# One step's 440 stages in another order: an interleaved image block on one core

## What is computed

```python
x = x + conv_block(_ln_c(x), ...)       # per 32 channels: 3x3 depthwise conv, silu, selective scan
                                        # in one of four directions, layernorm, gate, projection
t = _to_tokens(x)                       # 2304 tokens of 128 channels per image
t = t + ffn(_ln_t(t), ...)              # 16 experts; each takes its 288 best tokens (top_k)
x = _from_tokens(t, x)
```

## Time and profile before

| what | value |
|---|---|
| median of three runs | 2730.52 us |
| lowest, highest | 2722.64, 2745.78 us |
| span of the profiled execution | 2733.1 us |
| instructions in it | 41803 |
| mean granted TensorE clock, of full speed | 0.857 |

### The profile page before, as it was taken

How to read it: one execution, slowest core, us unless ns; L and a number is a source line. 1 busy time by engine, 2 the same in 40 slices (tenths; PEclk the granted TensorE clock), 3 DMA queues, 4 the chain that set the end, 5 groups by cost and what they waited for, 6 DMA issues and landing times.

```text
span 2733.1 us, 41803 instructions
## 1 busy us (share of the span) xinstructions
PE 2003.1 (73%) x12104; PEld 1220.3 (45%) x12104; DVE 1763.1 (65%) x4446; ACT 1620.9 (59%) x3141; POOL 1581.4 (58%) x1169
## 2 busy tenths in 40 slices
PE   3777788787877788786877788778878787765452
PEld 1333345454445454444545454445445454444331
DVE  2478787767676687757677777757676777664000
ACT  2456576756666576756666576757666576644221
POOL 0000366667575666757575766657575766676773
PEclk8999899999898998989898999988998998765555
DMA  3031334453635354453635454453635454444332
GB/s 109 28 89 48 83 71 93 85 130 71 139 72 126 73 108 81 87 124 72 140 72 116 85 110 79 96 120 71 138 72 127 78 110 81 79 70 81 52 64 53
DMA packets 275584, 244.85 MB, mean 90 GB/s; under 512 B 46240, under 2 KB 245264, under 8 KB 273040
## 3 DMA queue, kind: packets, MB, share of 16 engines
q0 software_dynamic: 101376, 80.29, 22.0%
q1 hardware_dynamic: 173968, 161.69, 21.0%
HBM read 83.71 MB, written 99.16 MB: 67 GB/s over the span
## 4 chain that ended last, share of the span: by engine, by line
issue 22%; DMA 15%; PE 15%; POOL 14%; SPq 10%; DVE 9%; ACT 9%; another core or an unknown queue 1%; POOLq 0%; DVEq 0%; ACTq 0%
POOL acc_dram L1035 8%; SPq L931 8%; DMA acc_dram<-Y,IDA 6%; POOL G L1016 5%; DMA slots_dram<-IX 4%; DVE hots L1437 3%; PE psum L1561 3%; PE psum L1586 2%; PE psum L1779 2%; DMA G<-rows_dram,IDX 2%; DMA GM<-rows_dram,IDX 2%; POOL acc_dram L1045 1%; SPq L964 1%; ACT hots L1168 1%; DMA LR<-slots_dram 1%
## 5 line engine op out<-in xcount | busy, mean ns | idle before, releaser
L1035 POOL DMA_INDIRECT acc_dram<-Y,IDA x512 | 860.5, 1681 | 394.3 <-issue 173.7
L1016 POOL DMA_INDIRECT G<-rows_dram,IDX x512 | 544.8, 1064 | 526.8 <-issue 429.3
L1437 DVE TENSOR_SCALAR_CACHE_REDUCE hots<-A,cand 96x384 f32<-96x384 f32 x720 | 401.7, 605 | 39.9 <-ACT A L1157 32.1
L1773 PE MATMUL psum<-m_all,G 128*128 128x128 f32 x512 | 127.9, 338 | 270.6 <-DMA G<-rows_dram,IDX 191.0
L1177 ACT ACTIVATE XG<-psum 128x256 f32<-128x256 f32 x256 | 97.5, 381 | 301.0 <-PE psum L1773 281.2
L1548 DVE TENSOR_TENSOR Y<-psum,GT 128x256 f32<-128x256 f32 x256 | 107.3, 419 | 258.7 <-PE psum L1790 206.8
L1561 PE MATMUL psum<-U,m_all 128*128 128x384 f32 x576 | 230.8, 532 | 27.3 <-DVE U L1364 17.6
L1779 PE MATMUL psum<-XG,w1s 128*128 128x256 f32 x512 | 209.1, 497 | 40.1 <-ACT PH L1202 19.6
L1561 PE MATMUL psum<-SQ,m_all 128*128 128x384 f32 x576 | 223.6, 517 | 18.8 <-ACT SQ L1074 10.0
L1045 POOL DMA_INDIRECT acc_dram<-YM,IDM x64 | 109.8, 1716 | 188.1 <-DMA acc_dram<-Y,IDA 100.5
L1773 PEld LDWEIGHTS psum<-m_all,G 128*128 128x128 f32 x512 | 65.1, 167 | 342.1 <-issue 248.2
(11 more groups left out here) (205 smaller groups left out, 4724.2 us busy)
## 6 DMA issues: line engine op xcount, KB each, us to landing
stack<-XS SPq DMA_DIRECT2D x384, 100.0 KB
rows_dram<-XT SPq DMA_DIRECT2D x16, 1296.0 KB, 7.9
X<-in_x SPq DMA_DIRECT2D x16, 1152.0 KB
acc_dram<-XT SPq DMA_DIRECT2D x16, 1152.0 KB
FT<-acc_dram SPq DMA_DIRECT2D x96, 192.0 KB
out<-OT SPq DMA_DIRECT2D x96, 192.0 KB
DH<-XS SPq DMA_DIRECT2D x96, 100.0 KB
DU<-XS SPq DMA_DIRECT2D x96, 100.0 KB
```

The lines of the kernel that those rows point to most:

```text
L1016: nc.gpsimd.indirect_dma_start(G[e % NG][:, c, :], None, rows_dram[of], bass.IndirectOffsetOnAxis(IDX[of][:, col:col + 1], 0)).then_inc(ga ...
L1035: nc.gpsimd.indirect_dma_start(acc_dram, bass.IndirectOffsetOnAxis(IDA[of][:, col:col + 1], 0), Y[e % NY][:, c, :], None, compute_op=ALU.a ...
L1437: last = v.tensor_scalar((GT1, EQ1, P1)[i], A[:], cand[:, i + 1:i + 2].bitcast(F32), 0.0, ALU.is_ge, ALU.add, accum_out=cnt[:, i:i + 1])
L1773: last = nc.tensor.transpose(bank6[:, c * FULL:(c + 1) * FULL], G[j % NG][:, c, 0:C], M["IDENT"])
```

## The change

On PE, all six parts of `conv(0)`, `layer2(0)` and `affinity_turn` now stand ahead of `conv(1, 0)`; on ACT the three `xs` stand together. The calls themselves, cut to places of which the above speaks (the full diff moves nearly every line):

```diff
+    q.lg_scale(s)
+    q.lg_shift(s)
+    q.lg_exp(s)
+    q.lg_norm(s)
+    gather(3)
     m.conv(s, 0, 0)
     m.conv(s, 0, 3)
-    q.lg_scale(s)
-    q.lg_shift(s)
...
+    gather(5)
+    scatter(3)
...
+    gather(7)
     m.dbu(s, 0)
...
-    fetch(5)
...
-    gather(15)
-    flip(4)
-    flipped(4)
-    m.tokens(s, par, 0)
-    q.store_rows(s, par)
...
     m.xm_turned(s, par, 0)
+    m.xm(s, par, 0)
+    m.xm_turned(s, par, 1)
+    q.store_rows(s, par)
...
+    scatter(12)
+    layer1(13)
+    scatter(13)
+    scatter(14)
+    scatter(15)
```

More of the change, by code:

```diff
@@ L373, in step @@
-    q.ahead(s, 4)
-    total(4)
-    m.delta(s, 0)
+    turn(2)
     decide(4)
-    m.z(s, par, 1, 0)
     q.count(s, 5, ka)
     q.ahead(s, 5)
-    m.u(s, 2)
-    m.du(s, 0)
[L382 to L386, removed]
+    m.zs(s, 1)
+    layer1(0)
+    before(0)
+    turned(2)
+    m.z(s, par, 2, 0)
+    m.du(s, 0)
     total(5)
     decide(5)
-    m.zs(s, 1)
+    layer2(2)
+    weigh(2)
+    m.z(s, par, 2, 1)
+    m.zs(s, 2)
+    q.count(s, 6, ka)
@@ L411, in step @@
+    turn(3)
+    turned(3)
+    rest(0)
+    total(7)
+    raw(0)
+    gather(5)
+    scatter(3)
+    turn_mixed(1)
+    turned_mixed(1)
+    m.spread_b(s, 0)
+    m.clamp(s, 2)
+    m.soft(s, 2)
+    q.ahead(s, 7)
+    decide(7)
+    m.delta(s, 1)
+    q.count(s, 8, ka)
+    layer1(3)
+    before(3)
+    turn(4)
+    gather(7)
     m.dbu(s, 0)
-    turn(3)
-    decide(7)
-    tables()
     m.decay(s, 0)
[L416 to L427, removed]
     layer1(2)
-    raw(0)
-    m.du(s, 1)
     before(2)
[L432 to L439, removed]
     total(8)
     turned(4)
+    layer1(4)
+    blend(0)
+    m.spread_b(s, 1)
+    q.ahead(s, 8)
+    decide(8)
     gelu(0, 2)
-    blend(0)
+    m.du(s, 1)
+    layer2(4)
+    m.scan(s, 0)
@@ L444, in step @@
+    q.count(s, 9, ka)
     summed(0)
+    scatter_mixed(0)
     m.spread_c(s, 0)
-    decide(8)
+    weigh(4)
     m.delta(s, 2)
[L448 to L453, removed]
     total(9)
-    q.ahead(s, 9)
-    weigh(4)
     layer2(5)
     m.spread_b(s, 2)
[L459 to L465, removed]
+    fetch(0)
+    gather(6)
     k2 = m.bank7()
     m.fc2(s, k2)
-    m.decay(s, 2)
+    q.ahead(s, 9)
@@ L487, in step @@
+    m.decay(s, 2)
+    m.scan(s, 1)
+    raw(1)
+    q.affinity_rows(s)
     layer1(5)
+    before(5)
+    m.sq2(s, 0)
     q.count(s, 11, ka)
-    m.sq2(s, 0)
-    raw(1)
-    m.scan(s, 2)
[L492 to L505, removed]
+    turn(6)
+    m.spread_c(s, 2)
+    scatter(4)
+    turn(7)
+    turned(6)
@@ L605, in step @@
-    turn(11)
-    before(9)
-    f.xn(nxt, other, 0)
-    kg = q.bank7()
-    q.slots_pe(s, 0, kg)
-    f.cen1(nxt, other, 2)
-    m.g(s, 2)
-    fetch(3)
+    m.g(s, 2)
+    kh0 = q.bank7()
+    q.hot(s, 0, kh0)
+    gather(13)
+    scatter(8)
+    layer2(10)
+    f.var1(nxt, 1)
+    layer1(9)
+    q.hot_scale(s, 0, kh0)
+    before(9)
+    blend(2)
+    kg0 = q.bank7()
+    q.slots_pe(s, 0, kg0)
+    weigh(10)
+    summed(2)
+    fetch(3)
+    turn(11)
+    f.xn(nxt, other, 0)
+    f.cen1(nxt, other, 2)
@@ L645, in step @@
+    turn(12)
+    turned(12)
+    gather(14)
+    layer2(11)
     layer1(12)
-    layer2(11)
+    gelu(2, 11)
+    rest(3)
+    kg1 = q.bank7()
+    q.slots_pe(s, 1, kg1)
     before(12)
-    kg = q.bank7()
-    q.slots_pe(s, 1, kg)
-    f.xs(nxt, other, 2)
-    gelu(2, 11)
-    m.xm_turned(s, par, 1)
-    m.xm(s, par, 0)
+    scale_mixed(3)
+    f.stack(nxt, other, 0)
+    weigh(11)
+    raw(3)
     m.xm_turned(s, par, 2)
+    m.xm(s, par, 1)
+    q.slots_sum(s, 1, kg1)
+    scatter(10)
+    m.xm(s, par, 2)
@@ L655, in step @@
     m.cen3(s, 0)
[L656 to L658 removed]
+    m.sq3(s, 0, last)
     m.cen3(s, 1)
[L660 to L680 removed]
+    gather(15)
@@ L724, in step @@
+    summed(3)
+    turned(14)
+    turn(15)
+    before(13)
+    turned(15)
+    m.xt(s, 0)
+    m.tokens(s, par, 1)
     m.xt(s, 1)
-    turned(14)
+    layer1(14)
+    before(14)
+    m.tokens(s, par, 2)
     m.stats(s, 0)
-    m.tokens(s, par, 2)
     m.stats(s, 1)
     m.xt(s, 2)
+    m.stats(s, 2)
+    layer1(15)
+    before(15)
+    put(4)
+    flip(5)
+    flipped(5)
+    gelu(3, 15)
+    tables()
     ks = q.bank7()
     q.slots_turn(s, ks)
-    turn(15)
-    turned(15)
     q.columns(s, par, ks)
-    layer1(14)
+    gather(16)
```

362 lines of the change are left out of this document (169 added, 193 removed).

## The result

The changed kernel takes 2521.23 us (median of 4 runs, 2515.39 to 2525.55) against 2730.72 us for the kernel before (4 runs, 2722.64 to 2745.78): a ratio of 0.923, 95% interval 0.920 to 0.926. That is 209 us less. The forecast was 2593, 140 us under the profiled span of the kernel before.

A forecast was written before the change was run, and what follows sets the result against it. No engine is busy all through a step; about 9 us in its middle and some 20 us at its end are lost to waiting. Sum: 2733 - 99 (end) - 66 (middle) + 25 (new waits) = 2593 us, range 2500 to 2724.

The forecast's parts named there:

- the two places: Waits in the middle and at the end of each step, about 9 us and some 20 us lost.
- the end: End of the step: xt's wait for the rows store goes, 7.1 us a step, 99 us; bounds 34 and 127.
- the middle: PE's and DVE's stall behind gather(6) shrinks, 5.5 us a step, 66 us; bounds nothing and 106.
- new waits: Small waits for stages a little late in PE's strict order: 25 us lost, possibly nothing or as much again.
- the rest: Steps 16 to 18, without conv block: scatter_mixed's gains by covers offset the bare scatters' losses, counted as nothing.
- My second chain: Tokens' chain to slots_turn: loses xt's 7.1 us wait; hot_scale(2), 2.49 us, now stands ahead of rstd3(0).
- c: Time from one bare scatter to the next on POOL before gather(16), taken as 7.85 us between 6.0 and 10.4.
- the formula 3c - 20.2: New middle stall per step in us if bare scatters hold gather(16): nothing below c = 6.7, 3.3 at 7.85.
- If gather(16) and the search come earlier by the same amount: Middle: gather(6) then comes 13 us earlier for the search and the 8.77 us stall is gone.
- my own list: Signs against the forecast: first count to hot(2) stays 112 us, new PE wait each step, end over 38 us.
- That of the slower kernel: Rival: bare scatters on POOL land slower still, 2786 us at c = 13.5; chance 0.1.
- All of it: Rival: both stalls, middle and end, go and nothing new comes, 2500 us; chance 0.13.

The follow-up runs named there:

- SP's order alone: Kernel before with only SP's stages in the new order (rows store ahead of the stacks, slots store right behind the second): 2637.0 us, ratio 0.964.
- the order of PE, ACT and DVE alone: Kernel before with only the stages of PE, ACT and DVE in the new order, SP and POOL in the old: 2735.9 us, ratio 1.000.
- POOL's order alone: Kernel before with only POOL's stages in the new order (gathers ahead of scatters' landings, scatters 12 to 15 before gather(16)): 2645.2 us, ratio 0.967.
- SP and POOL: Kernel before with the stages of SP and POOL in the new order, PE, ACT and DVE in the old: 2591.1 us, ratio 0.947.
- changed, gather(16) earlier: Changed kernel with gather(16) ahead of scatter(15) and gather(17) ahead of scatter_mixed(3) on POOL: 2495.9 us, ratio 0.912.

## Why the prediction was right, and where not

The sign, the range and the two places were right; the gain was 209 us where 140 were forecast. By stretches of the profiled execution, which gained 219: the end was to give 99 us and gave 149; the middle was to give 66, less 25 for new waits, and gave 61; the rest was to give nothing and gave 9. So the term that was most mis-sized is the end of the step, and half of what it gave was not in my sum.

*The end, up to slots_turn.* 373 to 300 us are 72 us, or 4.8 a step where I took 7.1, inside the bounds of 2.4 and 9.1. `xt`'s wait went and the slots store landed in 3 us, as said. What the sum had wrong is whose gain this is. "In the new order the rows store has gone ahead of the stacks", and with that I gave it to SP. SP's order alone does give 100 us, but that this is the forecast's figure is luck: its end wins 133 us and its middle loses 40. On top of POOL's order SP's is worth 54, on top of that of PE, ACT and DVE 71, and on top of both 17. I listed where `xt` went on ACT and priced `hot_scale(2)` there, but did not ask whether `xt` would still have to wait. It would not, and that alone wins nothing in this stretch: `turn(15)` then waits for gather(15), which goes out beside the rows store, and with SP's order too this wait is gone. Over the fifteen steps PE's busy time there is 328 of 372 us at a clock of 0.85 with the order of PE, ACT and DVE alone, and 280 of 293 at 1.00 with SP's order too. So 48 of these 79 us are PE's own time at another clock, a cost that my sum did not have. With POOL's order, gather(15) is issued 5 to 8 us ahead of the end of `hot(2)` instead of 7 to 10 behind it, and the stretch is 343 us without SP's order.

*The end, from slots_turn to the first count.* My second chain stopped at `slots_turn`; behind it I priced nothing. It gave 77 us, the largest single part. The order of PE, ACT and DVE alone brings this stretch from 238 to 164 us, SP's alone to 210, POOL's alone to 225. On PE `turn(15)`, layers 1 and `flip(5)` have gone from behind `slots_turn` to in front of it, and `affinity_turn` has gone ahead of conv(1, 0). Undoing the latter brings 45 of the 77 us back in this stretch. How the rest divides was not tried.

*The middle.* Gather(6) 43 us behind gather(16) was forecast, and 42.1 is the mean of 13 steps. c was taken as 7.85 us and is 6.5 on the mean in the changed kernel; with POOL's order and the rows store in its old place it is 7.6. At 6.5 the formula 3c - 20.2 gives no stall, and `hc` has none. But "If gather(16) and the search come earlier by the same amount" did not come true, and the formula, which lets gather(16) be held, has the first count too late. Means of 13 steps, in us:

| kernel | slots_turn to gather(16) | gather(16) to gather(6) | first count to gather(6) |
|---|---|---|---|
| before | 2.2 | 56.7 | 43.0 |
| SP's order alone | 2.1 | 57.9 | 45.7 |
| POOL's order alone | 9.1 | 47.1 | 40.7 |
| PE, ACT, DVE alone | 2.2 | 52.9 | 43.9 |
| SP and POOL | 13.8 | 45.8 | 46.2 |
| all: the changed kernel | 8.6 | 42.1 | 39.8 |
| changed, gather(16) earlier | 2.6 | 46.8 | 38.3 |

Behind `slots_turn` the first count comes 5.1 us earlier (10.9 us, 16.0 before) and gather(16) 6.4 us later, since it stands behind four bare scatters. So from `slots_turn` to gather(6) only 8.2 us are won of the 14.6, and from the first count to gather(6) 3.2. The formula took the first count as far behind `slots_turn` as before; with the c that was measured it has gather(6) 34.6 us (15.1 + 3c) behind the first count, and it is 39.8. With gather(16) ahead of scatter(15) another 25 us go.

*New small waits.* 25 us were taken. `over` waits 91.4 us against 72.3 and `turn_mixed` 98.8 against 37.8, and the stretch from the last count to `hot(2)` grows from 631 to 673 us (its part of the middle). The steps are 137 us long on the mean of 11, under the 140 to 146 forecast. By my own list, a new wait of several us in each step was to prove the forecast wrong; it did not, since removing it wins nothing.

*What held the step.* The forecast added terms. The runs show that they don't add: 100, 92 and 1 us alone, 209 together. A shorter end starts the search earlier, and with POOL's old round the middle is then longer: by 40 us under SP's order, where gather(6) comes 2.7 us later behind the first count, and by 79 under that of PE, ACT and DVE. In the latter gather(6) comes only 0.9 us later; PE's waits for gathers are longer (220.1 us for G, 81.6 for GM), and PE's busy time in the middle goes from 1294 to 1360 us as its clock goes from 0.94 to 0.90. POOL's order takes most of this away, and so is worth 92 us by itself and 144 on top of the other two. It does not take all: on top of it SP's order shortens the end by 106 us and lengthens the middle by 52, with gather(16) at 13.8 us behind `slots_turn`. Why the order of PE, ACT and DVE then brings it to 8.6 is not shown by a run of its own.

*The rivals.* That of the slower kernel needed c of 12 or more; the largest seen with POOL's order alone is 10.8, beside the rows store. "All of it", at 2500, came nearest, but for another reason than its own: neither term reached its bound, and the missing 77 us made up for it.

## What to carry to other kernels

When several in-order engines share one round, find the chain that an edit does not shorten (here from `slots_turn` by way of gather(16) to gather(6) on POOL) and price every other gain only up to what that chain lets through: an edit that wins nothing alone may be worth 70 us once the chain is shorter. Measure such a chain from the point that starts both sides, not from its first stage: 14.6 us were won from gather(16) on, and 6.4 of them lost in front of it. For a wait that goes, ask which of the edits removes it by itself, and what the same transfer delays next. And follow a moved stage to the next point where the step starts again, not to the first wait that it releases.

## What the runs showed of the hardware

A scatter that is in flight when the 1296 KB rows store is issued holds the next one for 9.8 to 10.8 us in 11 of 13 steps (POOL's order alone; the store goes out 2 to 3 us behind the scatter), against 5.9 to 6.1 for the one after it. The time of the issue seems to count: with the rows store put back in the changed kernel, it goes out 2 to 4 us ahead of scatter(12) in ten of steps 3 to 13, and the next scatter follows after 6.0 to 7.6. Beside twelve stack copies of 100 KB, which SP issues from 957.82 to 965.41 in the changed kernel's step, it was 6.3; I had priced stacks and store alike, between 6.0 and 10.4 (and the row with 10.4 has a gather between its two scatters, that with 6.0 has none).

The forecast had weighed a rule of the Trainium skill ("DMA: Bandwidth & Descriptors", section "Issuing engines are not separate DMA queues"): transfers of different engines interleave on the same 16 DMA engines. The traces agree with it for the rows store, with the 10.7 us above. That c would therefore stay at 10.4 does not follow, and did not happen: the changed kernel issues the rows store at 921.65, 26 us ahead of scatter(12) at 948.03, and c is 6.5. Whether the store weighs more than the stacks because it is one large transfer, or because it goes to DRAM like the scatters, was not tried.

The granted clock followed the waits. In the end of the step it was 0.76 and is 1.00 and 0.91; the mean is 0.857 before, 0.889 after, and 0.833 with the order of PE, ACT and DVE alone, whose time is that of before. PE's busy time goes with it, 2003.1, 1940.5 and 2068.6 us for the same 12104 matmuls. In one stretch its price can be read, 23.4 us at 0.79 against 18.5 at 1.00 for as many matmuls (the order of PE, ACT and DVE without and with SP's). How much of the 209 us is this and not the waits themselves stays open: no run held the clock.
